# Solve residuals from three bf16 pieces of the matrix, and the solution as a sum of three terms on GpSimd and VectorE

## The reference

```
state = state * d_t
delta = (v_t - k_t . state) * b_t
state = state + outer(k_t, delta)
o_t   = q_t . state
```

## Time and profile before

| what | value |
|---|---|
| median of 3 runs | 1804.15 us (1802.18 to 1804.24) |
| the profiled execution's own time | 1804.3 us |
| span of the trace (first to last instruction) | 1802.3 us |
| mean granted TensorE clock | 0.982 |
| TensorE busy | 1703.3 us (95%) |
| VectorE busy | 1316.0 us (73%) |
| ScalarE busy | 1167.9 us (65%) |
| GpSimd busy | 652.5 us (36%) |

### The profile page before, as it was taken

The page is one execution under the profiler, slowest core; times in us unless marked ns, Lnnn a source line. Parts: engine busy times, 40 slices in busy tenths (PEclk is TensorE's granted clock), DMA queues, the critical chain, the costliest instruction groups (busy, mean ns, idle before and its releaser), DMA issues.

```text
span 1802.3 us, 34261 instructions
## 1 busy us (share of the span) xinstructions
PE 1703.3 (95%) x13208; PEld 1322.5 (73%) x13208; DVE 1316.0 (73%) x2293; ACT 1167.9 (65%) x2185; POOL 652.5 (36%) x474
## 2 busy tenths in 40 slices
PE   7899999999998987999999999999999999999986
PEld 5676766767665666787787787877877877878875
DVE  7788888888866267767768767777677687677753
ACT  3335353443535465778878878887787788788762
POOL 2222213222214063615516426336246165163340
PEclk9999999999999997999999999999999999999998
DMA  3111010101103200110110101101101201111000
GB/s 138 35 55 47 33 67 33 67 33 55 46 1 105 76 19 1 37 59 25 37 56 28 36 25 60 36 25 37 59 25 36 60 25 36 38 47 36 7 2 24
DMA packets 51447, 75.16 MB, mean 42 GB/s; under 512 B 3392, under 2 KB 41792, under 8 KB 51312
## 3 DMA queue, kind: packets, MB, share of 16 engines
q1 hardware_dynamic: 51312, 73.28, 12.6%
HBM read 72.03 MB, written 1.25 MB: 41 GB/s over the span
## 4 chain that ended last, share of the span: by engine, by line
PE 54%; ACT 7%; DVE 6%; issue 3%; DVEq 0%
PE bank L731 12%; PE bank L911 7%; PE bank L751 5%; PE bank L866 4%; PE bank L789 3%; PE bank L802 2%; PE bank L816 2%; PE bank L812 2%; DVE d_sil L1334 2%; ACT d_dec L1133 2%; PE bank L874 2%; PE bank L887 2%; PE bank L854 2%; PE bank L888 2%; PE bank L889 2%
## 5 line engine op out<-in xcount | busy, mean ns | idle before, releaser
L1634 POOL TENSOR_TENSOR d_dec<-d_dec,d_qk 128x384 f32<-128x384 f32 x128 | 138.8, 1111 | 638.4 <-DVE d_N L1359 571.3
L1334 DVE SCALAR_TENSOR_TENSOR d_sil<-d_pre,d_w,d_sil 128x1024 f32<-128x1024 f32 x192 | 295.2, 1538 | 10.1 <-ACT d_pre L1099 9.9
L731 PE MATMUL bank<-xnT,d_w 128*128 128x512 f32 x480 | 242.4, 617 | 0.0
L189 PE MATMUL bank<-xnT,a_w 128*128 128x512 f32 x512 | 236.6, 596 | 0.0
L1380 DVE CAST_PREDICATED d_X<-tables_sb,bank 128x512 bf16<-128x512 int32 x192 | 134.3, 700 | 89.9 <-PE bank L802 76.4
L1396 DVE TENSOR_TENSOR d_Rb<-d_V,bank 128x512 bf16<-128x512 f32 x128 | 86.5, 685 | 109.8 <-PE bank L866 109.8
L489 POOL TENSOR_TENSOR a_hidc<-a_hid,a_comb 128x512 f32<-128x512 f32 x32 | 44.4, 1387 | 295.0 <-DVE a_hid L336 295.0
L189 PEld LDWEIGHTS bank<-xnT,a_w 128*128 128x128 f32 x512 | 90.6, 192 | 78.5 <-issue 78.5
L1161 ACT ACTIVATE d_T<-bank 128x512 bf16<-128x512 f32 x160 | 100.5, 628 | 65.2 <-PE bank L812 62.6
L866 PE MATMUL bank<-d_W,d_N 128*128 128x128 f32 x1024 | 130.6, 281 | 2.0 <-DVE d_W L1401 1.9
L508 ACT ACTIVATE a_sg<-a_sm 128x384 f32<-128x384 f32 x64 | 33.0, 515 | 152.0 <-DVE a_sm L341 152.0
(11 more groups left out here) (210 smaller groups left out, 4274.8 us busy)
## 6 DMA issues: line engine op xcount, KB each, us to landing
d_dec<-decay_scratch SPq DMA_DIRECT2D x32, 512.0 KB, 5.7
a_w<-w SPq DMA_DIRECT2D x16, 897.0 KB, 4.6
d_w<-w SPq DMA_DIRECT2D x16, 776.0 KB, 4.6
a_comb<-comb_scratch SPq DMA_DIRECT2D x16, 512.0 KB, 5.6
d_dec<-decay_scratch SPq DMA_DIRECT2D x32, 256.0 KB, 6.1
d_wo<-w SPq DMA_DIRECT2D x16, 256.0 KB, 3.1
f_w<-w SPq DMA_DIRECT2D x8, 256.0 KB, 4.2
x_sb<-x SPq DMA_DIRECT2D x2, 512.0 KB, 4.4
```

What stands on the lines that cost most here:

```text
L189: last = pe.matmul(psum[bank][:, :], wq(slot, part, k), xnT[:, k, half * HALF:(half + 1) * HALF], start=(k == 0), stop=(k == KT - 1))
L731: last = pe.matmul(psum[bank][:, :], cols(slot, (c * KT + k) * P, P), xnT[:, k, h * HALF:(h + 1) * HALF], start=(k == 0), stop=(k == KT - 1))
L1334: dve.scalar_tensor_tensor(sil[c][:, :, :], pre[c % 2][:, :, tap:tap + S], cols(slot, OC + 4 * c + tap, 1), sil[c][:, :, :], ALU.mult, ALU ...
L1634: pool.tensor_tensor(g, g, qk[b][:, :, :], ALU.mult).then_inc(s["p_done"], 1)
```

## The change

The matrix `N` (with its -1 diagonals) is taken apart into three bf16 pieces: `Nh` is `N` rounded (a ScalarE pass, `high`), `Nm` is the rest rounded and `Nl` the rest of that (GpSimd passes, `middle` and `lowest`). `Nl` takes the place of `Nb`, so `lowest` has to wait until TensorE has read `Nb` in the last level of the inverse. `residual` then works on bf16 operands alone. For `a` = 0 it sums two products in PSUM, with `Nh` and `Nm` on the bf16 first term `W0b`; for `a` = 1 it adds three more to the same sum, `Nl` on `W0b` and `Nh` and `Nm` on the bf16 change `dWb`. That is 8 and 12 bf16 matmuls for each `v`, where there were 4 and 4 in float32. `apply` no longer sums in PSUM, so the solution is `W0b + dWb +` the third result: GpSimd adds the first two (`partial`, four passes for each head), VectorE adds the third (`total`, four passes), and from the sum `Wv` the link and the outputs are computed as before. The first copy to `Wv` and the second become bf16 copies `first_w` and `change`; the third is gone. GpSimd's `mask` is cut in two halves and the second is put behind `lowest`; on ScalarE, three of the four groups of exponentials now stand in one row behind the second square.

```
-                for b in range(B):
-                    last = pe.matmul(psum[5 + 2 * v][:, b * P:(b + 1) * P], N[v][:, b, 2 * c, :], Wv[v][:, b, c, :],
-                                     start=True, stop=True)
+                    pe.wait_ge(s["nl_done"], i * 2 + v + 1)
+                    pe.wait_ge(s[f"dw_done{v}"], i * 2 + c + 1)
+                    parts = ((Nl, W0b), (Nh, dWb), (Nm, dWb))
+                for n, (coef, vec) in enumerate(parts):
+                    for b in range(B):
+                        last = pe.matmul(psum[5 + 2 * v][:, b * P:(b + 1) * P], coef[v][:, b, c, :], vec[v][:, b, :],
+                                         start=(a == 0 and n == 0 and b == 0), stop=(a == 1 and n == 2), skip_group_check=True)
...
+            def high(i, v):
+                act.wait_ge(s["diag_done"], i * 2 + v + 1)
+                act.activation(Nh[v][:, :, :, :], N[v][:, :, 0:3:2, :], ACT.Copy).then_inc(s["nh_done"], 1)
...
-                next_w(i, 0, 1)
+                change(i, 0)
                 if nxt:
                     square(ni, 1)
-                    batch_decays(ni, ns, 0)
-                    batch_decays(ni, ns, 1)
-                next_w(i, 0, 2)
-                if nxt:
-                    batch_decays(ni, ns, 2)
+                    for b in range(3):
+                        batch_decays(ni, ns, b)
...
+            def total(i, v, c):
+                dve.wait_ge(s["apply_ready"], i * 12 + 6 * c + 4 + v + 1)
+                dve.wait_ge(s["wsum_done"], i * 4 + 2 * c + v + 1)
+                dve.tensor_tensor(Wv[v][:, :, c, :], Wv[v][:, :, c, :], psum[4 + 2 * v][:, :].rearrange("p (b d) -> p b d", b=B),
+                                  ALU.add).then_inc(s[f"wup_done{v}"], 1)
...
+            def middle(i, v):
+                pool.wait_ge(s["nh_done"], i * 2 + v + 1)
+                rest = N[v][:, :, 0:3:2, :]
+                pool.tensor_tensor(rest, rest, Nh[v][:, :, :, :], ALU.subtract).then_inc(s["mid_done"], 1)
+                pool.wait_ge(s["mid_done"], i * 2 + v + 1)
+                pool.tensor_copy(Nm[v][:, :, :, :], rest).then_inc(s["nm_done"], 1)
+            def lowest(i, v):
+                pool.wait_ge(s["nm_done"], i * 2 + v + 1)
+                pool.wait_ge(s["x_ready"], i * 12 + 2 * len(LEVELS) - 2 + v + 1)
+                pool.tensor_tensor(Nl[v][:, :, :, :], N[v][:, :, 0:3:2, :], Nm[v][:, :, :, :],
+                                   ALU.subtract).then_inc(s["nl_done"], 1)
+            def partial(i, v, c):
+                pool.wait_ge(s["w0_done"], i * 4 + 2 * c + v + 1)
+                pool.wait_ge(s[f"dw_done{v}"], i * 2 + c + 1)
+                pool.tensor_tensor(Wv[v][:, :, c, :], W0b[v][:, :, :], dWb[v][:, :, :], ALU.add).then_inc(s["wsum_done"], 1)
...
+                for v in range(2):
+                    diagonal(i, v)
                 if nxt:
-                    mask(*nxt)
+                    mask(*nxt, 0)
+                for v in range(2):
+                    middle(i, v)
+                for v in range(2):
+                    lowest(i, v)
+                if nxt:
+                    mask(*nxt, 1)
+                for c in range(2):
+                    for v in range(2):
+                        partial(i, v, c)
                 if isinstance(i, int) and i == 0:
                     f_tail()
```

More of the change, by code:

```diff
@@ L631, in layer1_phase @@
         Wv = [m.sb(f"d_W{v}", [P, B, 2, P]) for v in range(2)]
+        Nh = [m.sb(f"d_Nh{v}", [P, B, 2, P], BF16) for v in range(2)]
+        Nm = [m.sb(f"d_Nm{v}", [P, B, 2, P], BF16) for v in range(2)]
+        Nl = Nb
+        W0b = [m.sb(f"d_W0b{v}", [P, B, P], BF16) for v in range(2)]
+        dWb = [m.sb(f"d_dWb{v}", [P, B, P], BF16) for v in range(2)]
         ysq = [Wv[v][:, :, :, :].rearrange("p b c d -> p (b c) d") for v in range(2)]
@@ L854, in apply @@
                     last = pe.matmul(psum[4 + 2 * v][:, b * P:(b + 1) * P], TT[v][:, 2 * b + c, :], Rb[v][:, b, :],
-                                     start=(a == 0 and b == 0), stop=(a == 2), skip_group_check=True)
+                                     start=True, stop=True)
                 last.then_inc(s["apply_ready"], 1)
@@ L1506, in body @@
                             f_scale()
-                        if a:
-                            update(i, c, a)
+                        if a == 1:
+                            change(i, c)
+                        elif a == 2:
+                            for v in range(2):
+                                total(i, v, c)
                         for f in mid[k]:
@@ L1613, in _, with mask @@
         def _(pool):
-            def mask(j, slot, i):
+            def mask(j, slot, i, v):
                 pool.wait_ge(dec_in[slot], j * 64 + 64)
-                for v in range(2):
-                    for c in (0, 2):
-                        g = dec[slot][v][:, :, c, :]
-                        last = pool.tensor_tensor(g, g, tabs["future"].unsqueeze(1).broadcast_to([P, B, P]), ALU.add)
-                    last.then_inc(s["mask_done"], 1)
+                for c in (0, 2):
+                    g = dec[slot][v][:, :, c, :]
+                    last = pool.tensor_tensor(g, g, tabs["future"].unsqueeze(1).broadcast_to([P, B, P]), ALU.add)
+                last.then_inc(s["mask_done"], 1)
             def scale_y(i, v):
@@ L1682, in _ @@
                     pool.tensor_copy(Xp[lv][:, v, :, :], identb[:, :].unsqueeze(1).broadcast_to([P, 8, P])).then_inc(ev["ident_done"], 1)
-            mask(0, 0, 0)
+            for v in range(2):
+                mask(0, 0, 0, v)
             loop(pool, body)
```

47 lines of the change are left out of this document (24 added, 23 removed).

## The result

The changed kernel takes 1838.37 us (median of 4 runs, 1837.80 to 1847.59) against 1803.16 us (4 runs, 1800.60 to 1804.24) for the kernel before on the same chip: a ratio of 1.0209, interval 1.0175 to 1.0244. It is slower by 35 us; I had predicted 1841. The profiled execution took 1837.8 us, its span 1835.55, 33.26 us more than the 1802.29 of before.

What follows compares the result with a forecast made beforehand. TensorE was taken to bound the kernel, with thin cover in chunk 0. Heads 1 to 14 gave +35.7, head 0 +2, head 15 -1: +36.7 on 1804.3, 1841 us; 8-in-10 range 1798 to 1872.

Steps and rivals of the forecast that it cites:

- The walk: Instruction-by-instruction timing of head 8's solve: outputs start 2.6 us later; 1841 us in total, 52 in 100.
- The rule of the hold: GpSimd passes and VectorE's taps exclude each other by instruction; a held tap ends about 1.08 us behind the pass.
- What is removed: TensorE's residual products: 32 float32, 7.36 us, become 80 bf16, 4.6 us; at most 2.8 us a head.
- Prices: Added passes: GpSimd subtraction 2.35 us (bounds 1.90 and 2.76), cast 1.04, `partial` 1.27; ScalarE's `high` nothing.
- The failed step: Chunk 0 ahead of the link: tap and first `partial` due at 1273.9; second `partial` ends at 1277.5.
- Chunk 1: Second chunk of the solve, GpSimd idle and no tap standing: shorter products give back 0.65 us.
- A head: Heads 1 to 14 each cost 2.55 us more, 35.7 us in all.
- the falls of the clock: Rival: TensorE's clock falls ahead of the link in each head, 28 us more, 1869 us; 18 in 100.
- Head 0: First head, its three long passes moved behind the last `partial`: +2 us, bounds -3 and +8.
- GpSimd in time: Rival: chunk 0's second `partial` ends by 1275.2; 1804 us at the turning point, 1784 if taps fall between passes; 20 in 100.
- Arithmetic alone: Rival: TensorE bounds the kernel and all 44 us of products come out, 1760 us; 1 in 50.
- The signs: Right: solve taps 1.6 to 2.9 us, waits naming GpSimd's sum before `total`; wrong: middle-head clock under 1.00, among others.

Runs made afterwards that it cites:

- experiment 1: The kernel before, with the passes of `high`, `middle` and `lowest` added, their results unused, and the mask cut in two around them: 1817.1 us.
- experiment 2: The changed kernel without the `middle` and `lowest` passes, all residual products using `Nh`; `partial` and `total` stay: 1799.4 us.
- experiment 11: The changed kernel with the five VectorE taps in the solve cut to 128x8, the rest of them left out: 1780.8 us.
- experiment 12: The kernel before with the same five VectorE taps in the solve cut to 128x8, the rest left out: 1797.5 us.
- experiment 5: The changed kernel with two bf16 pieces instead of three: one subtraction writes `Nm`, no cast, no `lowest`, no product with `Nl`: 1802.4 us.

## Why the prediction was right

The direction, the place and the time were right. The walk's steps were partly too long and partly too short, and one that I had as a rival came in part.

- **The rule of the hold** was right and decided the case: experiments 1, 2, 11 and 12 show it, and the taps' mean of 1894 ns for 1538 ns (the rows by line above). Operations with an input in PSUM kept their 0.69.
- **What is removed**: 57 ns a product held (four groups at 0.22 to 0.23 us), and TensorE's work fell. But "2.8 us a head" as the most that can come out was far from what can: with the taps of the solve all but gone 1.67 come out of it, and 1.07 of the head, since 0.53 are lost to a held tap ahead of the first residual (experiment 11). The shorter first residual moved the next apply by 0.44 us (1.40 from 1210.93 to 1212.33, before 1.84), since a wait of 0.33 for `left_over`, which the long products had covered, came to light; in experiment 11 the link comes 0.77 us sooner and chunk 1 gives 0.37.
- **Prices**: the subtraction takes 2.13 us, not 2.35; cast 1.04 as priced; `partial` 1.13 (2.26 for two), not 1.27; all inside the bounds. `high`, costed at nothing, cost nothing (experiment 5).
- **The walk, counted from the mark, predicted and measured in the common head**: first `middle` 7.8 and 7.77; both `Nm` done 16.7 and 15.1; `lowest` done 21.3 and 20.2; third tap done 22.4 and 22.6; second `left_over` 24.5 and 24.7; both `partial` done 29.3 and 26.9; both `total` done 30.1 and 29.2; link's sums 31.3 and 30.3. Up to the second `left_over` the walk is good to 0.2 us where it counts. The cheaper subtraction reversed one order: the second `middle` began at 1203.60, 0.3 us ahead of the tap, and held it, where I had let the tap in first. That tap (2.89 us) put off a copy of the inverse behind it, and the first residual started 0.54 us late, which I had not counted. The failed step is `partial`: "the next tap and the first partial are due together: tap 1275.2, partial 1276.3, second partial 1277.5". The mask's second half was through at 23.7 from the mark, for 25.7; so `partial` got in first and both were through 2.4 us sooner, and in the common head no `total` waited for GpSimd; it was the tap behind that was held (2.09). In two heads, 4 and 14, the second `total` did wait 0.52 us for `partial`; they are the ones with +1.39 and +1.42.
- **The link** is therefore 1.76 us late on TensorE (2.2 at VectorE's sums), not 3.2. The gaps that I gave as 1.5 and 1.4 are 1.29 and 0.80.
- **Chunk 1** gives back nothing (10.45 us from link to outputs, before 10.48), not 0.65: waits for `change`, `left_over` and `total` of 0.17 to 0.56 take the place of the products.
- **A head** costs 1.77 us, not 2.55. That is 11 us less than the sum over 14 heads, and the falls of the clock, left out of the sum and held for "likely some heads", put 9.4 back: 4 heads by 2.34. Two errors cancelled; the time of 1841 is better than its terms.
- **Head 0** is +2.65 for +2, head 14 +1.42 for 2.55, and what lies behind the mark of head 15 -2.5 for -1.
- **The rivals**: GpSimd in time was true in all but two heads (there `partial` was 0.52 us late), and yet VectorE's row was longer than before; the condition was right and the consequence wrong, since I had asked only whether `partial` is late and not whether it holds the tap ahead of `total`. The clock fell in 4 heads of 13. Arithmetic alone was rightly given next to nothing.
- **The signs** were mixed, as is to be expected where two errors cancel. The lengths of the taps and the 57 ns came. The waits did not name GpSimd's sum in front of `total` (but for two heads), TensorE idled 0.80 us and not 1 to 2 in front of the link, the subtractions (2.13) lay under 2.2 to 2.5, and a clock under 1.00 in middle heads, which I had named as a sign of being wrong, came in four.

## What to carry to other kernels

Before work goes to GpSimd because it is idle, look at what VectorE has in the same stretch: here every tap (two inputs in SBUF) that was issued under a GpSimd pass waited for the end of that instruction, and the queue of short PSUM operations behind the tap was late with it. Move such taps out of the stretch, or end the passes ahead of it: two pieces, the sum in PSUM and another order of three taps made 1778 us of 1838. And when the bound engine's work is cut, price the chain between its steps, not its busy time: of 2.8 us of products, 1.67 us came out of the solve with next to no taps in it, and none with them.
